# First attention: GpSimd's clipping pass also subtracts the maximum, and one exponential takes a pair of heads

## The reference, cut to what matters

```python
q = (query @ Wq + bq).reshape(B, Nq, H, D).transpose(0, 2, 1, 3)   # H = 16, D = 16
k = (key_value @ Wk + bk).reshape(B, Nkv, H, D).transpose(0, 2, 1, 3)
v = (key_value @ Wv + bv).reshape(B, Nkv, H, D).transpose(0, 2, 1, 3)
attn = jnp.einsum('bhqd,bhkd->bhqk', q, k) * scale
attn = jnp.clip(attn, -CLAMP, CLAMP)            # CLAMP = 10000
attn = jax.nn.softmax(attn, axis=-1)
x = jnp.einsum('bhqk,bhkd->bqhd', attn, v).reshape(B, Nq, Cq)
return x @ Wo + bo
```

## Time and profile before

| | us |
|---|---|
| median of 3 runs (827.2 to 830.2) | 829.48 |
| profiled execution, its time | 829.89 |
| profiled execution, its span | 827.8 |

### The profile page before, as it was taken

The page is one execution under the profiler, slowest core; times in us unless marked ns, Lnnn a source line. Parts: engine busy times, 40 slices in busy tenths (PEclk is TensorE's granted clock), DMA queues, the critical chain, the costliest instruction groups (busy, mean ns, idle before and its releaser), DMA issues.

```text
span 827.8 us, 16419 instructions
## 1 busy us (share of the span) xinstructions
PE 732.7 (89%) x5029; PEld 592.6 (72%) x5030; DVE 377.9 (46%) x1142; ACT 417.8 (50%) x977; POOL 273.4 (33%) x362
## 2 busy tenths in 40 slices
PE   3997899997179999699997999997889999999996
PEld 2775666666167888466665677774659999999995
DVE  4223677774321110677675445456654343333432
ACT  2445899995123323355554766664424443444442
POOL 5112555551420000212123111100236666757662
PEclk9997999998579999799999999998699999999999
DMA  5125000002718831110101111120025444443431
GB/s 129 40 80 192 2 2 2 2 2 69 267 30 293 274 133 32 43 33 23 32 5 53 44 48 62 46 78 0 1 66 158 116 126 118 125 122 113 133 116 40
DMA packets 60417, 67.31 MB, mean 81 GB/s; under 512 B 6050, under 2 KB 51336, under 8 KB 60380
## 3 DMA queue, kind: packets, MB, share of 16 engines
q1 hardware_dynamic: 57404, 63.29, 24.7%
q10 hardware_dynamic: 1952, 1.91, 0.7%
q0 software_dynamic: 1024, 1.64, 0.7%
HBM read 53.68 MB, written 7.22 MB: 74 GB/s over the span
## 4 chain that ended last, share of the span: by engine, by line
PE 70%; DVE 9%; ACT 8%; issue 5%; DMA 4%; POOL 2%; SPq 1%; DVEq 0%; POOLq 0%; ACTq 0%
PE psum L659 5%; PE psum L1944 5%; PE psum L1946 5%; PE psum L1945 5%; PE psum L1229 4%; PE psum L1242 4%; ACT probs L887 4%; PE psum L713 3%; PE psum L550 3%; PE psum L1959 3%; PE psum L1960 3%; PE psum L1958 3%; PE psum L564 3%; PE psum L698 3%; PE psum L826 2%
## 5 line engine op out<-in xcount | busy, mean ns | idle before, releaser
L2068 DVE TENSOR_TENSOR kT_all<-kT_all 128x400 f32<-128x400 f32 x60 | 36.7, 612 | 114.8 <-ACT kT_all L2002 106.5
L2041 POOL TENSOR_TENSOR h_low<-v_all,h_high 128x400 fp32r<-128x400 f32 x60 | 63.2, 1054 | 65.7 <-ACT h_high L2006 65.6
L1944 PE MATMUL psum<-xT_high,we_high 128*128 128x400 f32 x240 | 83.3, 347 | 0.3 <-DVE v_all L2073 0.3
L1946 PE MATMUL psum<-xT_high,we_low 128*128 128x400 f32 x240 | 82.8, 345 | 0.0
L1945 PE MATMUL psum<-xT_low,we_high 128*128 128x400 f32 x240 | 82.6, 344 | 0.0
L887 ACT ACTIVATE probs<-probs,negmax 100x361 f32<-100x361 f32 x128 | 68.9, 587 | 10.7 <-POOL probs L932 10.6
L2032 POOL TENSOR_TENSOR we_low<-v_all,we_high 128x512 fp32r<-128x512 f32 (+1 forms) x61 | 66.7, 1105 | 14.5 <-ACT we_high L1991 11.0
L940 DVE TENSOR_SCALAR_CACHE_REDUCE probs<-psum 100x361 f32<-100x361 f32 x128 | 60.7, 531 | 19.1 <-PE psum L816 19.1
L826 PEld LDWEIGHTS psum<-ident,probs 100*128 100x128 f32 (+1 forms) x384 | 39.7, 157 | 27.7 <-issue 19.9
L826 PE MATMUL psum<-ident,probs 100*128 100x100 f32 (+1 forms) x384 | 48.2, 264 | 11.5 <-ACT probsT L895 4.9
L2002 ACT ACTIVATE kT_all<-psum 128x400 f32<-128x400 f32 x60 | 30.0, 501 | 52.5 <-PE psum L1946 52.5
(11 more groups left out here) (357 smaller groups left out, 1673.6 us busy)
## 6 DMA issues: line engine op xcount, KB each, us to landing
v_all<-in_L_ffn_W_dram SPq DMA_DIRECT2D x16, 1024.0 KB, 7.8
kT_all<-coefT_dram SPq DMA_DIRECT2D x30, 400.0 KB, 3.6
vs<-v_all SPq DMA_DIRECT2D x8, 512.0 KB
v_all<-in_L_ffn_Wg_dram SPq DMA_DIRECT2D x31, 128.0 KB, 2.2
v_all<-in_L_ffn_Wu_dram SPq DMA_DIRECT2D x31, 128.0 KB, 2.2
v_all<-in_L_ffn_Wd_dram SPq DMA_DIRECT2D x31, 128.0 KB, 2.1
ctx_nat<-in_ctx_dram SPq DMA_DIRECT2D x17, 192.0 KB, 2.5
xs_dram<-zeros SPq DMA_DIRECT2D x1, 2048.0 KB, 7.7
```

Source lines behind the costliest of these rows:

```text
L1944: nc.tensor.matmul(ps, we_high[p][:, col], xT_high[:, c, tok], start=(c == 0), stop=False)
L1946: last = nc.tensor.matmul(ps, we_low[p][:, col], xT_high[:, c, tok], start=False, stop=(c == 1))
L2041: nc.gpsimd.tensor_tensor(h1_low[p][:, tok], h1T[:, tok], h1_high[p][:, tok].bitcast(F32), ALU.subtract).then_inc(h1_ready, 1)
L2068: nc.vector.tensor_tensor(g_act[half], g_act[half], coef_rows[p][:, half * HT:(half + 1) * HT], ALU.mult).then_inc(coef_used, 1)
```

## The change

```diff
     def act_attend0(act):
         def exps(n):
             act.wait_ge(A0.clamped, 2 * n + 2)
-            for hh in range(2):
-                row = probs[:, n % NPB, hh, 0:NKV]
-                last = nc.scalar.activation(row, row, ACT.Exp, bias=negmax[:, n % NPB, hh:hh + 1])
-            last.then_inc(A0.exp_done, 1)
+            pair = probs[:, n % NPB, :, 0:NKV]
+            nc.scalar.activation(pair, pair, ACT.Exp).then_inc(A0.exp_done, 1)
...
             pool.wait_ge(A0.clipped, n + 1)
             nc.gpsimd.tensor_scalar(negmax[:, n % NPB, :], row_top[:, n % NPB, :], -1.0, -CLAMP, ALU.mult, ALU.max
                                     ).then_inc(A0.clamped, 1)
-            pair = probs[:, n % NPB, :, 0:NKV]
-            nc.gpsimd.tensor_scalar(pair, pair, CLAMP, -CLAMP, ALU.min, ALU.max).then_inc(A0.clamped, 1)
+            pool.wait_ge(A0.clamped, 2 * n + 1)
+            for hh in range(2):
+                row = probs[:, n % NPB, hh, 0:NKV]
+                last = nc.gpsimd.tensor_scalar(row, row, negmax[:, n % NPB, hh:hh + 1], 0.0, ALU.add, ALU.min)
+            last.then_inc(A0.clamped, 1)
```

## The result

| | before | after |
|---|---|---|
| median, us | 829.84 (4 runs, 827.2 to 831.96) | 931.76 (4 runs, 930.75 to 937.6) |
| span of the profiled execution, us | 827.8 | 929.4 |

The change makes the kernel slower by a factor of 1.124 (95% interval 1.119 to 1.130). Forecast were 833.8 us and a range up to 846. The sign of the point forecast was right and its size was not: 102 us in place of 4.

What follows compares the result with a forecast made beforehand. PE and ACT's copies set the 14.32 us batch; POOL at 1.58 us per pair makes it 14.71. Eight batches add 3.1 us and the ramp 0.8, so 829.89 becomes 833.8 us; range 827.5 to 846.

Steps and rivals of the forecast that it cites:

- What bounds the kernel before: First attention stage: PE's transposes and ACT's copies set the 14.32 us batch; without waits for exponentials about 14.1.
- The rival that ACT's 17.9 us come out in full: ACT's 13.13 of 14.32 us per batch all lie on the path, giving 812 us; chance 0.04.
- ACT's part: One exponential over 722 elements takes 0.79 to 0.80 us instead of 1.08 for two, 0.28 less per pair.
- The operand: In POOL's pass, one per-partition operand adds 62 ns, making 566 ns over 361 elements.
- the gaps: On POOL, 0.295 us from small instruction to first pass, then 0.075 after each of the two passes.
- q: POOL's time per pair of heads, from start to start: 1.17 us before, forecast 1.58.
- The rival that the operand costs no spacing: POOL's passes follow each other 0.58 us apart, 1.46 us per pair, only the ramp late: 830.5 us; chance 0.24.
- an element costs 0.793 ns and 361 take 504 ns: POOL's pass over one head before the operand's cost, priced from constant-operand rows of 2 and 722 elements.
- rival 4: POOL's pass with an operand is much dearer per element and POOL sets the pace: 846 to 867 us; chance 0.19.
- The upper bound: POOL's pass costs at most a two-input instruction's 965 ns at 361 elements, 2.38 us per pair, 867 us.
- The sum: The stage gets 3.9 us longer: 3.1 from 8 batches over POOL and 0.8 in the ramp.
- the way over POOL: Chain from PE's scores over DVE, POOL and the exponential back: 8.39 + 4q per batch, 14.71 us forecast.

Runs made afterwards that it cites:

- ACT's half alone: Kernel before with one exponential over the pair without bias, the row maximum not subtracted, POOL's one pass kept; 830.33 us, ratio 0.9983.
- the run with the column of 10000: Kernel before with POOL clipping each head by itself, upper limit read from a per-partition column, ACT as before; 837.43 us, ratio 1.0078.
- The two runs of this kind: Kernel before with POOL's clip split per head, ACT as before: two constants, 834.97 us; upper limit from a per-partition column, 837.43 us.

## Why the prediction was right or wrong

**What bounds the kernel before: right.** ACT looked fullest and was not the bound. ACT's half alone shortened the batch to 14.03 us, where I had about 14.1, and moved the stage by 1.5 us, where I had 2. The rival that ACT's 17.9 us come out in full is excluded.

**ACT's part: right for the instruction.** The exponential takes 805 ns against 802 from the two rows.

**The operand: right, the gaps: nearly.** The operand was put at 62 ns and costs 72. From the start of the small instruction to the first pass it is 0.33 us in the kernel after where it was 0.295, so the new wait and the small instruction cost 0.03 more. Between the two passes I had a gap of 0.075 us, and instead they overlap by a few hundredths (1.11 us for two of 569 ns with add and mult). That gives q = 1.51 where 1.58 was forecast. The rival that the operand costs no spacing is wrong: in the run with the column of 10000, a POOL pair takes 0.30 + 1.10 + 0.08 = 1.48 us, 0.16 more than with constants, so the 72 ns show in the spacing too. The span of L1376 gave the better price here than the start behind it.

**The step that failed** is, in *POOL*, the term "an element costs 0.793 ns and 361 take 504 ns". I read it from min and max and used it for add and min, as if the price hung on the shape alone. The pair of operations sets it: 3.36 ns per element against 0.793, at 361 elements 219 + 359 x 3.36 = 1425 ns and with the operand 1497, measured 1508. That is the sign of being wrong that the prediction had named, a pass over 0.65 us. Even for min and max the two rows were of two kinds, since the small instruction does mult and max: 361 elements of min and max take 490 ns, where I had 504. The mechanism of rival 4 was the right one, "much dearer per element" and then 8q per batch, though not its reason: the operand, which it names, costs 72 ns, and the pass is as dear per element without one. With the measured q of 3.40 its own formula gives 8 x (27.2 - 14.3) = 103 us, and the stage became 103.7 longer.

**The upper bound failed too.** I took a two-input pass (965 ns) as the far end for a pass with an operand. The pass was dearer than that by half. L625 and L2041 are another instruction with its own price, and so bounded nothing. No row of the trace before showed any tensor-scalar with an addition at full width, as the text said; 0.19 for that case was too little, and its end at 867 us was not an end.

**The sum came out near where its price was right, in part by luck.** With add and mult a pass takes 569 ns against 566, and the kernel lies at a ratio of 1.0044, 3.7 us above before; the sum had 3.9. So a small loss, and the forecast's sign, would have been right at that price too. But q was 1.51 and not 1.58, 0.28 us less per batch, and the formula for the way over POOL, 8.39 + 4q, is short by 0.2: with q of 1.51, 1.77 and 1.83 the batches take 14.65, 15.72 and 15.94 us, which is 8.6 + 4q each time. The two misses nearly cancel.

**The way over POOL had the right slope from a wrong picture.** I let four pairs follow each other on POOL without a stop, with one exponential on the way. The runs show POOL waiting for DVE ahead of each quad with q of 1.51, and ahead of nearly each with 1.83. The pace is set by a lap from the scores of a quad to those of the next but one, twice per batch, with two pairs and the exponential of the second one in each. That makes 4q too, but the exponential counts twice. With ACT's two exponentials left in place, a lap should then be 0.29 us longer (0.99 against 0.70 in the prediction) and a batch 0.58. The two runs of this kind take 14.55 and 15.10 us with q of 1.32 and 1.48, which is 9.2 or 9.3 + 4q. So ACT's half of the change, worth 0.3 us per batch beside POOL's cheap pass, is worth about 0.6, by this working, where the laps over POOL set the pace. By these formulas POOL alone decides from a q of about 2.15 on; no run lies between 1.83 and 3.03. At 3.03 and 3.40 the batches are 24.19 and 27.26, both 8q.

## What to carry to other kernels

The price of a tensor-scalar pass on POOL hangs on the operations in it, so a row for the same shape with other operations bounds nothing; measure the very pair of operations before building on it, and put a minimum ahead of a maximum in a clip. When work is moved onto an engine that seems idle, ask what a single item takes to pass through it and not how full it is: POOL had room for 6 us in a batch of 14.32, and each 0.1 us more per pair still cost 0.4 us per batch from a q of about 1.5 on, since the way from scores to scores passes it twice per batch, with two pairs each time. And before paying to relieve the fullest engine, look in the chain for the places where its work is really waited for; here that was one quad in four, 0.3 us.

## What the runs showed of the hardware

- POOL's tensor-scalar over float32 in SBUF has fast pairs of operations, min max, mult add, add mult and mult mult, 0.8 us over 722 elements, and the fourteen other pairs tried take 2.6 us. One operation alone takes 2.0. Why these four, no run shows. The constants of these runs leave the scores as they are; with real values there are add min (1508 ns over 361 elements) and add mult (569), which agree.
- One operand with a value per partition adds 72 ns to such an instruction (490 to 562 ns at 361 elements), and nothing that grows with the elements: add min grows by 3.38 ns per element with it and costs 3.36 without.
- An addition of a repeated column as a two-input instruction takes 1391 ns over 722 elements. That is less than one tensor-scalar addition of a constant (2.03 us) and more than two passes of add and mult with the column (2 x 569 ns).
- The granted clock falls to 0.50, the lower level of 1.2 GHz, at about 73 us in both kernels, behind a wait of PE of 1.59 us for ACT's `qT_all` (L600). Before, it is 1.00 again from 88 us on. After, where PE waits for ACT in nearly every quad, it is 0.50 until 129 us and 0.56 in the batches from there on (1.00 in the earlier trace rows); the page after, in slices of 23.2 us:

```profile
PEclk9995555555566569999899999999969999999999
```

A block of six transposes takes 1.25 us there against 0.72. While POOL set the pace the trace shows no cost of that. Behind POOL's last pass it may cost something: from its end to the last addition it is 10.28 us (292.81 to 303.09) against 8.87 before, and the projection L862 there takes 2.03 us against 1.11.

```profile
151.55 1.25 PE L826 MATMUL psum<-ident,probs 100*128 100x100 f32 x6 [1.45 <-ACT probsT L893]
```
